# Mamba and mixture-of-experts block: inflows moved to the end of their unit and held to the product two units back, scatters laid one to a unit

## What is computed

```python
x = x + block1(layernorm(x))      # block1: x + mamba(ln(x)), then a gated feed-forward
x = x + moe(layernorm(x))         # 8 experts, 2 per token

def mamba(u):                     # 256 inner channels, 16 states
    x_in, z = split(u @ in_proj.T)
    xc = silu(conv1d(x_in))                    # 4 taps
    dt, B, C = split(xc @ x_proj.T)
    delta = softplus(dt @ dt_w.T + dt_b)
    h_t = exp(delta_t * A) * h_(t-1) + delta_t * B_t * xc_t    # for each channel and state
    y_t = sum over states of C_t * h_t
    return ((y + xc * D) * silu(z)) @ out_w.T

def moe(t):
    w, e = top2(t @ Ws + bs); w = softmax(w)
    return sum_k w_k * (silu(t @ Wg[e_k]) * (t @ Wu[e_k])) @ Wd[e_k]
```

## Time and profile before

| | |
|---|---|
| median of 3 runs | 844.0 us (843.27 to 844.61) |
| the profiled execution | 846.1 us, of which the span is 844.3 us |
| granted PE clock, mean | 0.889 of full speed |
| DVE busy | 739.2 us, 88% |
| PE busy | 649.8 us, 77% |
| POOL busy | 581.2 us, 69% |
| ACT busy | 506.5 us, 60% |
| DMA engines | 36.3% and 3.0% (hardware and software queues), 118 GB/s |
| chain of waits, by engine | DVE 37%, PE 34%, issue 17%, ACT 7% |

### The profile page before, as it was taken

The page is one execution under the profiler, slowest core; times in us unless marked ns, Lnnn a source line. Parts: engine busy times, 40 slices in busy tenths (PEclk is TensorE's granted clock), DMA queues, the critical chain, the costliest instruction groups (busy, mean ns, idle before and its releaser), DMA issues.

```text
span 844.3 us, 12617 instructions
## 1 busy us (share of the span) xinstructions
PE 649.8 (77%) x3545; PEld 465.3 (55%) x3545; DVE 739.2 (88%) x1145; ACT 506.5 (60%) x1091; POOL 581.2 (69%) x487
## 2 busy tenths in 40 slices
PE   4438688878778877887877876886876789888991
PEld 2124445545355536764566635873554457788990
DVE  1376998989999999999999999999999897686774
ACT  2545795876688577464846577555854775444440
POOL 1094675677977797689958896789846994456451
PEclk9659899989989898997989988897887899999995
DMA  6923233223323336542464336532424621123247
GB/s 175 263 104 103 87 113 113 82 84 97 116 69 107 106 102 182 158 145 99 130 174 140 109 96 203 148 110 94 133 91 128 171 61 33 39 65 83 65 129 231
DMA packets 80248, 99.94 MB, mean 118 GB/s; under 512 B 10215, under 2 KB 48051, under 8 KB 80163
## 3 DMA queue, kind: packets, MB, share of 16 engines
q1 hardware_dynamic: 75859, 90.21, 36.3%
q0 software_dynamic: 4320, 8.92, 3.0%
HBM read 87.56 MB, written 15.35 MB: 122 GB/s over the span
## 4 chain that ended last, share of the span: by engine, by line
DVE 37%; PE 34%; issue 17%; ACT 7%; DMA 2%; POOL 2%; DVEq 1%; SPq 0%; ACTq 0%; POOLq 0%
DVE state L1077 18%; PE work_front L1248 4%; PE y L1288 4%; DVE product L1087 4%; PE up L1399 2%; PE work_front L1254 2%; PE y L1284 2%; PE up L1410 2%; PE gate L1392 2%; DVE stats L1007 2%; ACT decay L941 1%; DVE silu_m L1213 1%; PE gate L1313 1%; DVE arena L1052 1%; PE work_side L1332 1%
## 5 line engine op out<-in xcount | busy, mean ns | idle before, releaser
L818 POOL TENSOR_TENSOR inflow<-du,b_wide 128x1024 f32<-128x1024 f32 x128 | 315.5, 2468 | 145.0 <-DVE product L1087 92.0
L1077 DVE TENSOR_TENSOR_SCAN state<-decay,carry,inflow 128x512 f32<-128x512 f32 x192 | 234.7, 1264 | 6.5 <-ACT decay L941 6.5
L1087 DVE TENSOR_TENSOR product<-state,c_wide 128x1024 f32<-128x1024 f32 (+1 forms) x93 | 139.1, 1495 | 4.4 <-PE y L1284 3.3
L941 ACT ACTIVATE decay<-arena,a_neg 128x512 f32<-128x512 f32 x128 | 86.6, 688 | 60.7 <-DVE state L1077 56.9
L1284 PE MATMUL y<-ident,product 128*128 128x128 f32 x664 | 106.4, 305 | 20.6 <-DVE product L1087 20.5
L1284 PEld LDWEIGHTS y<-ident,product 128*128 128x128 f32 x664 | 87.2, 158 | 62.5 <-issue 34.7
L848 POOL DMA_INDIRECT y_dram<-y_rows,x_rows x71 | 82.5, 1162 | 56.0 <-ACT y_rows L997 49.1
L941 ACT ACTIVATE decay<-delta_odd,a_neg 128x512 f32<-128x512 f32 x128 | 86.6, 689 | 56.3 <-DVE state L1077 56.1
L1288 PE MATMUL y<-h_rows,ident 128*128 128x512 f32 x180 | 100.9, 652 | 7.0 <-ACT h_rows L906 6.5
L842 POOL DMA_INDIRECT row_dram<-m_tok,place x64 | 74.4, 1163 | 24.3 <-issue 12.7
L1077 DVE TENSOR_TENSOR_SCAN state<-decay,inflow 128x512 f32<-128x512 f32 x64 | 74.5, 1203 | 6.1 <-ACT decay L941 3.6
(11 more groups left out here) (232 smaller groups left out, 1342.6 us busy)
## 6 DMA issues: line engine op xcount, KB each, us to landing
b_wide<-bc_dram SPq DMA_DIRECT2D x128, 256.0 KB, 3.3
c_wide<-bc_dram SPq DMA_DIRECT2D x93, 256.0 KB, 3.5
w_stage<-gate_up_dram SPq DMA_DIRECT2D x26, 344.0 KB, 4.2
x_rows<-row_dram SPq DMA_DIRECT2D x71, 65.0 KB, 1.9
arena<-gate_up_dram SPq DMA_DIRECT2D x8, 344.0 KB, 4.4
x_tok<-in_x SPq DMA_DIRECT2D x8, 256.0 KB, 5.8
out<-x_tok SPq DMA_DIRECT2D x8, 256.0 KB, 4.8
inflow<-y_dram SPq DMA_DIRECT2D x6, 256.0 KB, 4.4
```

The costliest lines, as they stand in the source:

```text
L818: e.tensor_tensor(inflow[:, key % 3], du[:, c % 2], b_wide[:, key % ROW_SLOTS:key % ROW_SLOTS + 1, :].to_broadcast([P, HALVES, CHUNK]), AL ...
L941: e.activation(decay_bank[h][:], delta[c % 2][:, h, :], ACT.Exp, scale=a_neg[:, h, n:n + 1]).then_inc(S["decay"], 1)
L1077: e.tensor_tensor_scan(state[:, key % STATE_SLOTS, h, :], decay_bank[h][:], inflow[:, key % 3, h, :], 0.0 if c % (SEQ // CHUNK) == 0 else ...
L1087: e.tensor_tensor(product[:, key % 2, :, :wide], state[:, key % STATE_SLOTS, :, :wide], c_wide[:, key % ROW_SLOTS:key % ROW_SLOTS + 1, :wi ...
```

## The change

Two edits of the order and one that follows from them:

1. Inflow i + 2 is put at the end of unit i, behind product i, and no longer near its start. Its wait is for the product (or the scans) of unit k - 2, where it was k - 3.
2. `SEND` has one scatter to a table row, in n = 0 to 7; tag1 goes to n = 4, list0 to n = 5 (the 6th), list1 to n = 8 (the 9th), list2 to n = 9 (the 10th). `SEND_HELD` stays.
3. A chunk counts as `sent` from its last scatter on (n = 7), and as `listed` from list2 on (n = 9). A round's first row load is thus put in the list at n = 8, where it already stood, but now ahead of list2; its first two weight loads go from n = 8 and 9 to n = 10.

```diff
 SEND = [
-    ("tag0", ("scatter", 0, 0), ("scatter", 1, 0)),
-    (("scatter", 2, 0), ("scatter", 3, 0)),
-    ("list0",),
-    ("tag1", ("scatter", 0, 1), ("scatter", 1, 1)),
-    (),
-    (("scatter", 2, 1), ("scatter", 3, 1)),
+    ("tag0", ("scatter", 0, 0)),
+    (("scatter", 1, 0),),
+    (("scatter", 2, 0),),
+    (("scatter", 3, 0),),
+    ("tag1", ("scatter", 0, 1)),
+    (("scatter", 1, 1), "list0"),
+    (("scatter", 2, 1),),
+    (("scatter", 3, 1),),
     ("list1",),
     ("list2",),
 ]
...
             for name, key in sends.pop(0):
                 put(name, key)
+                if name == "scatter" and key[1:] == (SUB - 1, TOPK - 1):
+                    sent.add(key[0])
                 if name == "list2":
-                    sent.add(key)
                     listed.add(key)
...
         fetch("fetch_c", i + 2)
-        fetch("inflow", i + 2)
...
         put("times_c", i)
+        fetch("inflow", i + 2)
...
-                    if key >= 3:
-                        if share[key - 3] < SUB:
-                            e.wait_ge(S["times_c"], products[key - 3])
+                    if key >= 2:
+                        if share[key - 2] < SUB:
+                            e.wait_ge(S["times_c"], products[key - 2])
                         else:
-                            e.wait_ge(S["scan"], HALVES * (key - 2))
+                            e.wait_ge(S["scan"], HALVES * (key - 1))
```

## The result

| | before | after |
|---|---|---|
| median of 4 runs, us | 844.31 (843.27 to 846.16) | 853.70 (852.52 to 855.45) |
| profiled execution: time, span, mean granted clock | 846.1, 844.3, 0.889 | 855.45, 853.4, 0.884 |

The ratio is 1.0105, 95% interval 1.008 to 1.013: slower by 8.9 us (the two medians lie 9.4 apart), where +6.2 and 850.2 us had been forecast (range 841 to 857). The direction held. Of the four terms of the sum the first is about right; the other three are not.

What follows compares the result with a forecast made beforehand. The prediction took DVE plus its products' collisions with POOL's work as the bound. Terms 3.0 - 10.2 + 7.5 + 5.9 = +6.2 us gave 852.3 profiled, so a median of 850.2 us, range 841 to 857.

Steps and rivals of the forecast that it cites:

- The inflow's move: All chunks: POOL's slots in time stay, one unit of lead goes; gains nothing alone, costs nothing where POOL is on time.
- term 3: n = 3 to 9, chunks 2 to 6: POOL gets more work and scans wait for it; +7.5 us, bounds -14 and +19.
- Term 1: Chunk 7: with less lead, scan 125 starts 2.2 us later and scan 126 another 0.8; +3.0 us.
- Term 2: n = 0 to 2, chunks 2 to 6: fewer scatters let products n = 2 escape the inflow; -10.2 us, bounds 0 and -11.15.
- Term 4: n = 10, chunks 3, 5 and 6: inflow beside L1052 makes it 2.65 us, not 0.69; +5.9 us, bounds 0 and +5.9.
- A: Rival, n = 3 to 10: waits replace collisions, stretches take no longer, n = 10 stays clean; -7.2, 836.8 us; chance 0.25.
- B: Rival, SP's queue: loads come late, an inflow or PE waits 3 us in each of four rounds; 862 us; chance 0.07.
- The rule on who holds the port: Five stretches: if the first starter holds the pair, gate_h and xc precede the inflow; 0.4 us less each, 848.2; not taken.

Runs made afterwards that it cites:

- e2: Kernel before with the change's SEND table and `sent` marks, inflow placed and waiting as before: ratio 1.0044.
- e3: Changed kernel, but from unit 112 on (chunk 7) the inflow has its old place and waits for k - 3: ratio 1.0062.
- e1: Kernel before with the inflow's move alone, SEND table and marks as before: ratio 1.0160.
- e4: Kernel before, but from unit 112 on (chunk 7) the inflow has the new place and waits for k - 2: ratio 1.0045.
- e6: Kernel before with one scatter moved from n = 1 to n = 2 and list0 from n = 2 to n = 4: ratio 1.0028.
- e11: Changed kernel with list1 and list2 one unit later, row loads behind list2 again, jobs in n = 13 to 5: ratio 1.0094.
- e7: Kernel before with inflows filling only half their slot in n = 5 to 7 of chunks 4 to 6: ratio 0.9907.

## Why the prediction was right, and where it was wrong

The span grew by 9.1 us. By the trace's own marks this divides into: n = 2 products -9.65, the waits just ahead of them +1.6, the unit n = 3 +5.5, the stretches behind it to n = 9 +4.5, n = 10 +2.4, n = 11 to 15 -0.7, chunk 7 +4.9, tail +1.7, and head and chunk 0 -1.2. By the ratios of e2, e3 and the change (1.0044, 1.0062, 1.0105) the list of scatters with the old lead stands for 0.44%, the shorter lead outside chunk 7 for 0.2%, within the noise, and that of chunk 7 for 0.43%.

- **The inflow's move.** "This part alone gains nothing" is right (e1). That it costs nothing "where POOL is on time" is beside the point in chunks 3 to 6, where POOL is not: 9 to 10 us in sum with the old list. The prediction had this inside term 3.
- **Term 1, chunk 7: +3.0.** The mechanism is right: scan 125 waits 2.46 us, for the 2.2 said. It was undersized behind that: 0.8 us was given to scan 126, which lost 2.9. The working left out that inflows 126 and 127 would now stand side by side and hold the `w_stage` copy for 2 us. In the trace +4.9; in the times of e3 and e4 3.6 to 3.8, which does not exclude 3.0.
- **Term 2, n = 2: -10.2.** Right for the instruction (-9.65) and wrong for the time, and it is the step that failed. It took DVE's busy time for the bound and looked at no other engine in n = 0 to 3. Up to product n = 3 the 1.24 us came through in each of chunks 2 and 3, and 1.3 of 2.35 us in chunk 5. In chunks 4 to 6 together it is nothing: DVE -6.5 us, time -0.1. e2 and e6 show that such a gain is spent, at n = 3 or behind it. That PE, late by its work or by its lower clock, takes the part at n = 3 is read from the waits; no run took work off PE. (The words "with one scatter gone" do not give the 371.4 of the working: that is two scatters earlier, one from n = 0 and one from n = 1. The inflow came at 371.59.)
- **The unit n = 3.** No term had it. From product n = 2 to product n = 3 chunks 4 to 6 took 6.34, 6.43 and 6.43 us and now 8.59, 7.49 and 8.58. Ahead of product n = 2 another 1.0 and 0.6 us came in chunks 4 and 6.
- **Term 3, n = 3 to 9: +7.5.** 24.6, 31.7, 34.3, 33.9 and 32.9 us, for 24.6, 32.0, 35.15, 34.35 and 34.35: +4.5. Following POOL from price to price was right to 0.3 us in chunks 2 and 3. The scan that waits in chunk 4 is 71, as said, 2.96 us for 2.5 to 3; in chunks 5 and 6 it was the scans of both n = 6 and n = 7. In all the scans of chunks 4 to 6 wait 13.1 us, within the 10 to 20 said.
- **Term 4, n = 10: +5.9.** Wrong instruction and too large. The inflow meets L1051 (`series`, 2.24 us in chunk 4, for 1.19 before), and `small` takes 0.69 there, in all of chunks 3 to 6, where 2.65 had been said; the units n = 10 of chunks 3 to 6 gained and lost to +2.4 in sum. The prediction assumed that the inflow would keep its time against DVE's front steps; it comes a step earlier.
- **Rivals.** A, waits in place of collisions, happened in n = 4 to 6 of chunks 5 and 6, but new collisions (products n = 7 of 3.2 to 3.5 us) ate it. B: SP waits 29.5 us for lists, four times, and no inflow or gate shows a wait for it; e11, in which the loads stand behind the list again, is not faster.
- **The rule on who holds the port.** Product 88 of e2 begins at 499.76, the inflow at 499.98, and the product takes 3.65 us, the inflow its plain 2.35. The Trainium skill, SBUF — State Buffer, section "SBUF: two separate sides", says that whichever of the two engines' operations starts first has the pair for its whole instruction. Between product and inflow alone this trace does not agree, and neither does. But in both a scatter, also an operation of POOL, was still running when the product began (498.67 to 499.94 here, 372.87 to 373.83 there). If the scatter had the pair, the product never held it, and the rule is not contradicted; it only leaves open which of the two that wait gets the pair next, and here it was the inflow both times. No run separates these readings.

That the forecast 850.2 came near 853.7 is in part luck, since errors of both signs met: +7.1 (n = 3 and the wait ahead of product n = 2), +1.9 (term 1), +1.7 (tail) and +0.55 (term 2) against -3.0 (term 3), -3.5 (term 4), -1.2 and -0.7. The -1.2 and the +1.7 are no larger than what two traces of the kernel before differ by.

## What to carry to other kernels

Before a stretched instruction's excess is booked as time, cut the window in which it lies and read every engine's busy share and the granted clock in it: here DVE, PE and POOL were at 99, 90 and 89% in n = 0 to 3, and 6.5 us less of DVE gave nothing in sum. To find which engine pays, take work from one alone, even if the result is then another, and then read whether the others' busy time stayed: in e7 it did not, so the run parts less than it seems. Where two engines take turns, a unit of lead is what hides their unevenness; giving it up by itself cost 9 to 10 us over the four chunks in which both were full. And profile the unchanged kernel twice, so that the parts that differ by themselves are known.

## What the runs showed that was not expected

- All four kernels with the new lead in chunk 7 (changed, e1, e4, e11) leave PE idle for 4.34 or 4.35 us at the late scans, and in all four the granted clock falls to 0.50, the lower of its two levels, within 1 us of the end of that pause, for 3.4 or 6.8 us. In the ten traces with the old lead there PE is idle for 2.96 us at most, and the clock stays at 1.00. That this costs time is not shown: of three kernels on one chip e3, without the fall, has a tail of 150.1 us, e4 and e1, with it, 149.7 and 150.8.
- What a collision costs went with the inflow's length and not with the DVE step's: `w_stage` went from 0.48 to 2.57 us, `gate_h` from 0.68 to 3.00, a product from 1.22 to 3.65, all 2.1 to 2.4 us more. With half an inflow beside it the product n = 4 of chunk 5 took 1.57 us for 3.10.
- The unchanged kernel had chunk 1 at 77.2 and 74.6 us in its two traces, and chunks 3 to 5 alike to 0.1. In e4, which has the same order up to chunk 6, chunk 5 is 1.1 us off.
